# A graph layer on one core: the gathered rows of the first layer's second stretch split into two f32r terms

## The reference

```python
xn = _layernorm(x)
h = xn
for layer in range(6):
    agg = jax.ops.segment_sum(h[src], dst, num_segments=n)
    z = (h + agg) @ W1[layer] + b1[layer]
    z = relu(_batchnorm(z, g1[layer], be1[layer]))
    z = z @ W2[layer] + b2[layer]
    z = _batchnorm(z, g2[layer], be2[layer])
    h = z if layer == 5 else relu(z)
x = x + h + mix(xn)                  # per head: kv = k^T v / N, out = q @ kv
x = x + ffn(_layernorm(x))           # 8 experts, three products each
```

## Time and profile before

| | |
|---|---|
| runs of the kernel before | 4645.51 us median of 3 (4636.44 to 4645.72) |
| the profiled execution | 4649.79 us, its span 4648.0 us |
| PE busy | 4416.8 us (95%) |
| DVE, ACT, POOL busy | 66%, 67%, 64% |
| chain that ended last | PE 81%, DVE 6%, issue 4%, ACT 3%, POOL 3%, DMA 2% |
| second stretch of the first layer | about 534 to 830 us of the span |

### The profile page before, as it was taken

The page is one execution under the profiler, slowest core; times in us unless marked ns, Lnnn a source line. Parts: engine busy times, 40 slices in busy tenths (PEclk is TensorE's granted clock), DMA queues, the critical chain, the costliest instruction groups (busy, mean ns, idle before and its releaser), DMA issues.

```text
span 4648.0 us, 69554 instructions
## 1 busy us (share of the span) xinstructions
PE 4416.8 (95%) x18931; PEld 3240.2 (70%) x18931; DVE 3053.8 (66%) x7493; ACT 3113.4 (67%) x4297; POOL 2985.7 (64%) x3420
## 2 busy tenths in 40 slices
PE   4999999999999999899998999899998899999999
PEld 3666688588866888578875888568875766666665
DVE  6888766466665666656665666656665466666666
ACT  5767533488866888578876888578875555555555
POOL 5777766067771777447772777637773277777886
PEclk6999999999999999999999999999999799999999
DMA  6444644055543555255543555345555000000000
GB/s 227 156 138 151 214 153 142 26 194 172 171 137 121 179 174 170 81 176 174 171 148 112 176 173 163 114 141 176 179 159 177 10 1 8 8 8 8 8 8 8
DMA packets 198882, 571.18 MB, mean 123 GB/s; under 512 B 44498, under 2 KB 63420, under 8 KB 198396
## 3 DMA queue, kind: packets, MB, share of 16 engines
q0 software_dynamic: 109728, 299.78, 22.1%
q1 hardware_dynamic: 81404, 238.40, 14.6%
q10 hardware_dynamic: 7392, 28.90, 1.6%
HBM read 487.16 MB, written 79.74 MB: 122 GB/s over the span
## 4 chain that ended last, share of the span: by engine, by line
PE 81%; DVE 6%; issue 4%; ACT 3%; POOL 3%; DMA 2%; ACTq 0%; DVEq 0%; POOLq 0%; SPq 0%
PE bank L1064 35%; PE bank L1274 12%; PE bank L965 8%; PE bank L1283 7%; PE bank L1159 5%; PE bank L962 4%; PE bank L1093 4%; PE bank L1008 3%; POOL G L786 1%; ACT Z L1326 1%; DMA G<-y_table,idx 1%; PE bank L973 1%; DVE Gsp L1622 1%; DMA BIG<-y_table,idx 1%; POOL BIG L786 1%
## 5 line engine op out<-in xcount | busy, mean ns | idle before, releaser
L1064 PE MATMUL bank<-Ac,Ych 128*128 128x512 f32 x7644 | 1813.3, 391 | 0.7 <-DVE Z L1746 0.6
L786 POOL DMA_INDIRECT G<-y_table,idx x1416 | 1373.0, 970 | 540.7 <-issue 414.6
L1064 PEld LDWEIGHTS bank<-Ac,Ych 128*128 128x128 f32 x7644 | 1434.4, 188 | 304.2 <-DVE Z L1746 3.1
L1372 ACT CAST Ac<-BIG 128x2048 fp32r<-128x2048 uint8 (+1 forms) x546 | 913.2, 1689 | 361.8 <-PE bank L965 254.6
L786 POOL DMA_INDIRECT BIG<-y_table,idx x870 | 827.9, 952 | 266.4 <-issue 246.9
L1622 DVE TENSOR_TENSOR Gsp<-bank,Gsp 128x512 fp32r<-128x512 f32 x875 | 564.2, 684 | 490.0 <-ACT bank L1358 489.5
L1632 DVE TENSOR_SCALAR onehot<-iota,rel 128x128 fp32r<-128x128 f32 x2290 | 514.6, 300 | 180.3 <-PE bank L965 152.4
L2117 DVE TENSOR_TENSOR G<-G,bank 128x448 f32<-128x448 f32 x784 | 461.2, 618 | 216.4 <-ACT G L1544 114.6
L965 PE MATMUL bank<-Gsp,onehot 128*128 128x512 f32 x1750 | 497.9, 405 | 32.2 <-DVE Gsp L1622 32.0
L1549 ACT ACTIVATE G<-G,fsh,fsc 128x448 f32<-128x448 f32 x448 | 334.0, 757 | 251.8 <-DVE G L2117 246.4
L1746 DVE TENSOR_TENSOR Z<-Z,bank 128x512 f32 x546 | 373.8, 685 | 180.6 <-PE bank L1064 134.0
(11 more groups left out here) (231 smaller groups left out, 5874.0 us busy)
## 6 DMA issues: line engine op xcount, KB each, us to landing
BIG<-adjacency SPq DMA_DIRECT2D x273, 448.0 KB, 3.6
BIG<-y_table SPq DMA_DIRECT2D x27, 896.0 KB, 6.3
G<-y_table,idx POOLq DMA_INDIRECT x1416
y_table<-BIG SPq DMA_DIRECT2D x25, 896.0 KB, 3.8
adjacency<-BIG ACTq DMA_DIRECT2D x7, 3136.0 KB
BIG<-y_table,idx POOLq DMA_INDIRECT x870
BIG<-in_x SPq DMA_DIRECT2D x14, 896.0 KB, 8.8
y_table<-BIG ACTq DMA_DIRECT2D x7, 896.0 KB, 3.6
```

Source lines behind the costliest of these rows:

```text
L786: nc.gpsimd.indirect_dma_start(out=rows[:, j, :], out_offset=None, in_=y_table, in_offset=bass.IndirectOffsetOnAxis(ap=idx[:, t:t + 1], ax ...
L1064: last = mm(bank[2 * (k % 2) + b][:, 0:UW], Ych[pos % 2][:, i, s, b * P:(b + 1) * P], Ac[x_ % NAC][:, i - CA * h, :], start=(i == 0 and s ...
L1372: nc.scalar.copy(Ac[x_ % NAC][:, 0:t1 - t0, :], Land[k % NL][:, t0:t1, :]).then_inc(s_ac, 1)
```

## The change

From step 91 on, a quad of the first layer is split as in the later layers, but without the copy to PSUM: ScalarE casts the rows to f32r (high term), VectorE subtracts the high term from the rows, both operands in SBUF, and writes the low term over the rows. TensorE multiplies both terms with one matmul of 512 columns for a tile. A split quad takes twice the bytes of a raw one. So there are three places (`Gsp0`): the two halves of `G` that held two raw quads each, and the bytes of the third cast half. The dense part is left with two cast halves (`casts`). In a step TensorE now has the halves and the transposes ahead of the quad.

```diff
+        Gsp0 = Gsp[0:2] + [f32r_at("Gsp0x", [P, GJ, 2, D], BIG_AT + 2 * QUAD_BYTES)]
...
+        def place0(n):
+            return (N1 % RQ0 // 2, 1 - N1 % RQ0 // 2, 2)[(n - N1) % 3]
+        def last_there(n):
+            if n >= N1 + 3:
+                return n - 3
+            return max((m for m in range(N1) if place0(n) < 2 and m % RQ0 // 2 == place0(n)), default=None)
+        def casts(l):
+            return NAC - 1 if first_layer(l) else NAC
...
-                if n >= turn:
+                if first_layer(l) and n >= N1:
+                    if last_there(n) is not None:
+                        hold(pool, s_mmq, last_there(n) + 1)
+                    else:
+                        hold(pool, s_fl[(S - 1) % 2], (S - 1) // 2 * LANES + LANES)
+                elif n >= turn:
                     hold(pool, s_mmq, quads_before(l) + n - turn + 1)
...
-                if first_layer(l):
+                if is_split(l, n):
+                    pe.wait_ge(s_gl, split_before(l) + n + 1)
+                else:
                     pe.wait_ge(s_rows, there)
-                else:
-                    pe.wait_ge(s_gl, (l - 1) * N1 + n + 1)
...
+                if first_layer(l):
+                    nc.scalar.copy(split_place(l, n)[:, 0:tiles(n), 0, :], rows[:, 0:tiles(n), :]).then_inc(s_gh, 1)
+                    return
...
-                if x_ >= NAC:
-                    act.wait_ge(*dense_done(l, x_ - NAC))
-                if first_layer(l) and x_ == NAC - 1:
-                    act.wait_ge(s_fl[(S - 1) % 2], (S - 1) // 2 * LANES + LANES)
+                if x_ >= casts(l):
+                    act.wait_ge(*dense_done(l, x_ - casts(l)))
...
+                if first_layer(l):
+                    there = split_place(l, n)
+                    tt(there[:, 0:tiles(n), 1, :], gathered(l, n)[0][:, 0:tiles(n), :],
+                       there[:, 0:tiles(n), 0, :].bitcast(fp32), ALU.subtract).then_inc(s_gl, 1)
+                    return
...
-                if first_layer(l):
+                if first_layer(l) and g < NGR:
                     V.tensor_copy(grow[:, g % 2, :], group_bank(g)[:, 0:D]).then_inc(s_ev, 1)
```

More of the change, by code:

```diff
@@ L197, in gps_layer @@
         raw = [places[q // 2].rearrange("p (q j k f) -> p q j k f", q=2, j=GJ, k=2)[:, q % 2, :, 1, :] for q in range(RQ)]
+        Gsp0 = Gsp[0:2] + [f32r_at("Gsp0x", [P, GJ, 2, D], BIG_AT + 2 * QUAD_BYTES)]
+        raw_split = raw[0:2] + [at(2 * QUAD_BYTES, QUAD_BYTES).rearrange("p (j k f) -> p j k f", j=GJ, k=2)[:, :, 1, :]]
+        assert AC_BYTES >= QUAD_BYTES
         raw0 = [G[:, q * GJ * D:(q + 1) * GJ * D].rearrange("p (j f) -> p j f", j=GJ) for q in range(RQ0)]
@@ L289, in gps_layer @@
         s_g0 = [sem(f"s_g0{q}") for q in range(RQ0)]
+        s_gx = [sem(f"s_gx{q}") for q in range(len(Gsp0))]
         s_g = [sem(f"s_g{q}") for q in range(RQ)]
@@ L421, in loaded, with is_split, split_before, split_place @@
             return (len(first) + (l - 1) * len(later) + later.index(pos) + 1) * LANES
+        def is_split(l, n):
+            return not first_layer(l) or n >= N1
+        def split_before(l):
+            return -N1 if first_layer(l) else (l - 1) * N1 + N0 - N1
+        def place0(n):
[4 more added lines that the diff above has]
+            return max((m for m in range(N1) if place0(n) < 2 and m % RQ0 // 2 == place0(n)), default=None)
+        def split_place(l, n):
+            return Gsp0[place0(n)] if first_layer(l) else Gsp[n % RQ]
+        def casts(l):
+            return NAC - 1 if first_layer(l) else NAC
         def gathered(l, n):
+            if first_layer(l) and n >= N1:
+                q = place0(n)
+                return raw_split[q], s_gx[q], sum(tiles(m) for m in range(N1, n + 1) if place0(m) == q) * LANES
             if first_layer(l):
@@ L954, in quad @@
                 rows, s_rows, there = gathered(l, n)
-                if first_layer(l):
+                if is_split(l, n):
+                    pe.wait_ge(s_gl, split_before(l) + n + 1)
+                else:
                     pe.wait_ge(s_rows, there)
-                else:
-                    pe.wait_ge(s_gl, (l - 1) * N1 + n + 1)
                 for j in range(tiles(n)):
                     start, stop = first and j == 0, last_ and j == tiles(n) - 1
-                    if first_layer(l):
+                    if not is_split(l, n):
                         last = mm(group_bank(g)[:, 0:D], onehot[:, q, j, :].bitcast(fp32), rows[:, j, :],
@@ L965, in quad @@
                         last = mm(group_bank(g)[:, 0:2 * D], onehot[:, q, j, :],
-                                  Gsp[n % RQ][:, j, :, :].rearrange("p k f -> p (k f)"), start=start, stop=stop)
+                                  split_place(l, n)[:, j, :, :].rearrange("p k f -> p (k f)"), start=start, stop=stop)
                 last.then_inc(s_mmq, 1)
@@ L1064, in dense_half @@
                             last = mm(bank[2 * (k % 2) + b][:, 0:UW], Ych[pos % 2][:, i, s, b * P:(b + 1) * P],
-                                      Ac[x_ % NAC][:, i - CA * h, :], start=(i == 0 and s == 0), stop=(i == CT - 1 and s == 1))
+                                      Ac[x_ % casts(l)][:, i - CA * h, :], start=(i == 0 and s == 0), stop=(i == CT - 1 and s == 1))
                 if dense_done(l, x_)[0] is s_dn:
@@ L1114, in gather_stage @@
                 for n in range(quads(l)):
-                    if first_layer(l):
+                    if first_layer(l) and n < N1:
                         quad(l, n)
@@ L1124, in gather_stage @@
                     if first_layer(l):
+                        if n >= N1:
+                            quad(l, n)
                         if set_at(n, MIX_LAG) is not None:
@@ L1355, in quad_high @@
                 if n > 0 or not (isinstance(l, int) and l == 1):
-                    act.wait_ge(s_gl, (l - 1) * N1 + n)
+                    act.wait_ge(s_gl, split_before(l) + n)
                 for j in range(0, tiles(n), 2):
@@ L1365, in cast_half @@
                     act.wait_ge(s_ap[k % NL], (uses + k // NL + 1) * LANES)
-                if x_ >= NAC:
-                    act.wait_ge(*dense_done(l, x_ - NAC))
-                if first_layer(l) and x_ == NAC - 1:
-                    act.wait_ge(s_fl[(S - 1) % 2], (S - 1) // 2 * LANES + LANES)
+                if x_ >= casts(l):
+                    act.wait_ge(*dense_done(l, x_ - casts(l)))
                 t0, t1 = (0, CA) if h == 0 else (CA, CT)
-                nc.scalar.copy(Ac[x_ % NAC][:, 0:t1 - t0, :], Land[k % NL][:, t0:t1, :]).then_inc(s_ac, 1)
+                nc.scalar.copy(Ac[x_ % casts(l)][:, 0:t1 - t0, :], Land[k % NL][:, t0:t1, :]).then_inc(s_ac, 1)
             def evict_z1(l, i):
@@ L1466, in gather_stage @@
                             half(x_)
+                        quad_high(l, n)
                         if set_at(n, 1) is not None:
@@ L1618, in quad_low @@
             def quad_low(l, n):
[L1620 removed]
+                dve.wait_ge(s_gh, split_before(l) + n + 1)
+                if first_layer(l):
[3 more added lines that the diff above has]
+                    return
                 for j in range(0, tiles(n), 2):
@@ L1810, in gather_stage @@
                             build_one_hots(B)
-                    elif not first_layer(l):
+                    else:
                         quad_low(l, n)
```

2 lines of the change are left out of this document (removed).

## The result

| | before | after |
|---|---|---|
| median of 5 runs on one chip | 4642.51 us (4636.44 to 4645.72) | 4665.03 us (4663.88 to 4668.84) |
| ratio | | 1.0055, 95% interval 1.0041 to 1.0069 |
| profiled execution, its span | 4649.8, 4648.0 us | 4668.84, 4667.1 us |

The changed kernel is slower by 22.5 us. The forecast was 4653.5 us, 8 us more than the kernel before, its range 4638 to 4669, and slower was its likeliest sign by a little. The side was right; the time came 11.5 us above the forecast, and the change is 2.8 times the one forecast.

What follows compares the result with a forecast made beforehand. PE bound the kernel before; after the change DVE would, with a floor of 823.8 us plus 14 of hand-off waits, 837.8 against 830.35. That made 8 us more, 4653.5 us, range 4638 to 4669.

Steps and rivals of the forecast that it cites:

- PE's saving: First layer's split quads on PE: 0.91 us each against 1.73, 38.1 us less over 46.5 full quads.
- The start: Quads 91 to 94, ahead of the first mixing set: waits for places make DVE start it at 564.6, 14.7 us later.
- VectorE's own time: DVE behind the first mixing set: 203.6 us plus subtractions 49.0 and group sums 3.8, 256.4, then 2.8 for last sums and transposes.
- The waits at the hand-offs: Mixing sets: DVE waits for ScalarE's new cast queued behind the root, 1 us a set, 14 us in all.
- DVE, not PE, is the bound by 20 us: End of the stretch, first W1 product: DVE's floor without waits 823.8 us, PE's 803.2.
- Rival 4: PE slower by the clock: half clock after pauses at the start and before transposes, 22 us more, 4667; chance 0.13.
- the case that I thought likeliest: The changed stretch: DVE becomes the bound and hand-offs cost 5 to 23 us, 4653.5 us; chance 0.50.
- Rival 5: Slower by the three places: landings of 8 us lengthen a place's round, 23 us on top of 8, 4676; chance 0.08.
- Rivals 2 and 3: Rival 2: DVE bound, queues absorb the hand-offs, 4639 us, chance 0.17; rival 3: PE stays bound, 4618 to 4630, 0.07.
- Rival 6: DVE's subtractions held behind gather issues on POOL, 16.6 us on the bound engine, 4670 us; chance 0.03.
- The rule on ports: POOL's gather issues beside DVE's two-SBUF-input subtractions: the later one blocks; 13 us for 48 new ones, hidden, adding nothing.

Runs made afterwards that it cites:

- the run that took 6.4 us of PE's busy time away: The changed kernel with idle products of ones on TensorE before each group's transposes, four each, six before the first; ratio 1.0038 to the kernel before.

## Why the prediction was right or wrong

- **PE's saving**, 38.1 us: 19.5 in busy time. The count is right, and so is 0.91 us for a quad at the full clock; behind most pauses neither the quads nor the dense products ran at it.
- **The start.** From the end of quad 90 (531.2) to the first mixing set I had 30.8 us (533.8 to 564.6); 34.1 were measured. The chain of places was right. Missing is the gather's issue held for 4.29 us, which I had seen only as 1.89, beside one operation. Two smaller misses about cancel: the store 0.8 later, the landing of quad 94 about 4.2 us for 5.2.
- **VectorE's own time** behind the first set, 256.4 + 2.8 = 259.2 us, was right to 1%: 282.9 us less 26.3 of waits for cast and PE is 256.6. The subtraction took 1.23 us, and what followed it began 1.14 behind its start, which is the 1.15 of the forecast.
- **The waits at the hand-offs** are the term that was mis-sized: 14 us forecast (bounds 0 and 28), 26.3 measured. I had seen one cause, the cast behind the root. Moving the root away changed nothing; the cast also stands behind adjacency halves that wait for PE, and behind landings (24 us of ACT's waits in the kernel after). A wait priced by one queue was held by three. Added up, the first set came 0.7 later than 564.6, DVE's own time was 2.6 less, the waits 12.3 more: 10.4 us, which is 848.2 for the 837.8 of the sum.
- **"DVE, not PE, is the bound by 20 us"** held for the sign only. With 50.7 us of DVE's work gone, 46.2 of it behind the first set, 13.8 us came back there.
- **Rival 4** has the number that came (4667) and its sign, a clock below 1 after 560, is there (0.93). But the run that took 6.4 us of PE's busy time away won nothing. How much of the slow products lies on the path isn't settled: the chain of waits holds 24.5 us of products at 0.50 in the stretch, and 12.0 in the profile on the other chip, and half of that is what the clock can have cost there, 12 and 6 us. Part of the 11.5 us that I fell short may be it; it would then be inside the waits, not beside them.
- **The range.** 4665 lies outside the 4644 to 4662 of the case that I thought likeliest. That it lies within the whole range is owed to the width that rivals 4 and 5 gave it.
- **Rivals 2 and 3** are out: PE waits 26.1 us for the rows of groups. **Rival 5** in its form, landings over 6.5 us, did not occur (behind the first set, where ACT waited for a landing, the cast began 1.7 to 5.2 us after the quad's last issue; only quad 91 at the start took 6.5), but the three places are one of the circles. **Rival 6** is out: no subtraction took over 1.28 us, 1.23 in the mean.
- **The rule on ports.** POOL's issues took 187.6 us for 176 from 548 to 845, 1.07 each, 0.05 more than before (forecast 0.07) and hidden as forecast but for the start. The rule was that of the two the later one blocks while the first holds the ports. At 546.85 the issue started 0.09 us behind DVE and stayed held through eight DVE instructions, the last of which began 2.3 us after the issue did. As the Trainium skill ("SBUF — State Buffer", section "Who interferes with whom") puts it, whichever started first keeps the ports; the trace agrees for the first of the eight, and for the 42 held issues as far as they end 0.82 us after a DVE operation. For the other seven of the eight it shows DVE going ahead of an issue that had been waiting longer, which the twelve issues among other low terms don't.

Of the signs named ahead, these came: PE's waits for DVE over 30 us (48.9 with the start), DVE on PE under 15 (6.5), the subtraction at 1.22, split quads at 0.91 at the full clock, the first mixing set (565.3 for 564). Just missed were DVE's waits for the cast, 19.8 us for 20 to 35, and DVE's 234 us of 283 for 235 of 270. Missed were PE's busy time (255 us for 240), the first product with W1 (848 for 838) and the long issues of POOL: 31 above 1.1 us for 18, which is 1.7 times as many, not two to three.

## What to carry to other kernels

When work is taken from the bound engine and given to two others, count the buffers' circles as well as each engine's sum: an engine with a free third still comes late if its queue stands behind three kinds of waits. Shift less than the sums of busy time allow, and try a part: half of the groups, with a later start and another order, came out at 0.9994 of the kernel before, where all of them cost 0.35 to 0.55%. And price the start of a stage by itself, since 17.9 of 20.4 us were lost before the new pace counted. After one wait is removed, look at which wait took its place before calling it the cause.

## What the runs showed of the hardware

- An indirect gather's issue takes 0.95 us alone. All 42 of the changed kernel's stretch that took over 1.05 us, and all 24 before, end 0.81 or 0.82 us after a DVE operation with both inputs in SBUF; no such subtraction was longer for it (1.23 us in the mean, 1.28 at most).
- One such issue took 4.29 us, beside eight of these DVE operations in a row. Twelve others in the same trace that began among seven in a row took 0.94 to 1.03 us; why is open.
- Behind eight pauses of PE, of 2.25 to 15.5 us, the next split quad took 1.66 to 2.06 us for 1.07. With the root moved later, a quad behind a pause of 2.81 us took 1.18.
